# Reordering the loop body of four engine programs in an attention and low-rank feed-forward block

## Time and profile before

| | |
|---|---|
| median of 3 runs | 653.52 us |
| the profiled execution, its own time | 653.7 us |
| its span, first to last instruction | 651.7 us |
| mean granted TensorE clock, of full speed | 0.982 |
| PE busy | 608.7 us (93%) |
| DVE busy | 502.2 us (77%) |
| ACT busy | 418.3 us (64%) |
| POOL busy | 421.1 us (65%) |
| DMA, mean over the span | 32 GB/s |

### The profile page before, as it was taken

How to read it: one execution, slowest core, us unless ns; L and a number is a source line. 1 busy time by engine, 2 the same in 40 slices (tenths; PEclk the granted TensorE clock), 3 DMA queues, 4 the chain that set the end, 5 groups by cost and what they waited for, 6 DMA issues and landing times.

```text
span 651.7 us, 10353 instructions
## 1 busy us (share of the span) xinstructions
PE 608.7 (93%) x3437; PEld 522.9 (80%) x3437; DVE 502.2 (77%) x1093; ACT 418.3 (64%) x635; POOL 421.1 (65%) x363
## 2 busy tenths in 40 slices
PE   3699999999999999999999999999999999999996
PEld 1577878978798888878789788988798787987875
DVE  3457788797796968788796977968787877987567
ACT  0246685695668675695666856685756855677743
POOL 2745875677567765588566766587755785655664
PEclk9579999999999999999999999999999999999998
DMA  9201010210001000120002000020001200010001
GB/s 259 42 1 34 0 33 2 88 42 2 1 33 64 32 0 0 64 64 0 0 0 97 32 0 0 32 88 8 0 0 64 64 0 0 3 62 1 1 1 65
DMA packets 11745, 20.88 MB, mean 32 GB/s; under 512 B 3903, under 2 KB 7374, under 8 KB 11726
## 3 DMA queue, kind: packets, MB, share of 16 engines
q1 hardware_dynamic: 8144, 19.93, 8.8%
q10 hardware_dynamic: 3582, 0.70, 0.7%
HBM read 12.24 MB, written 8.39 MB: 32 GB/s over the span
## 4 chain that ended last, share of the span: by engine, by line
PE 45%; DVE 29%; ACT 10%; issue 8%; POOL 6%; ACTq 2%; DMA 1%; DVEq 0%; POOLq 0%
PE bank L1405 12%; PE bank L1411 6%; PE bank L1522 5%; PE bank L1577 5%; DVE fw L922 4%; DVE K L970 3%; PE bank L1497 3%; ACT fw L604 3%; PE bank L1478 3%; DVE st L892 2%; DVE hT L929 2%; POOL XNB L395 2%; PE bank L1488 2%; DVE XN L909 2%; DVE qT L977 2%
## 5 line engine op out<-in xcount | busy, mean ns | idle before, releaser
L252 POOL TENSOR_TENSOR gl<-fw,gh 128x512 fp32r<-128x512 f32 x80 | 106.4, 1335 | 60.5 <-ACT gh L609 59.5
L400 POOL TENSOR_TENSOR sqs<-fw 128x512 f32<-128x512 f32 x48 | 65.1, 1356 | 75.6 <-ACT fw L594 75.6
L604 ACT ACTIVATE fw<-fw,vec 128x512 f32<-128x512 f32 x96 | 76.1, 808 | 24.9 <-DVE fw L922 24.8
L594 ACT ACTIVATE fw<-bank,b1c 128x512 f32<-128x512 f32 x96 | 61.1, 685 | 41.5 <-PE bank L1411 40.5
L922 DVE SCALAR_TENSOR_TENSOR fw<-bank,b1c,rb 128x512 f32<-128x512 f32 x96 | 68.6, 743 | 12.4 <-ACT rb L600 12.4
L364 POOL TENSOR_TENSOR rsf<-vef,neghalf 128x4 f32<-128x4 f32 x48 | 51.3, 1069 | 33.0 <-DVE vef L915 32.9
L1533 PE MATMUL bank<-K,XN 128*128 128x256 f32 x256 | 61.8, 379 | 0.2 <-DVE K L970 0.2
L1577 PE MATMUL bank<-M,qT 128*128 128x256 f32 x256 | 60.7, 381 | 0.3 <-DVE qT L977 0.3
L364 POOL TENSOR_TENSOR rs<-ve,neghalf 128x2 f32<-128x2 f32 (+1 forms) x48 | 45.4, 945 | 24.1 <-DVE ve L1008 18.3
L609 ACT ACTIVATE gh<-fw 128x512 fp32r<-128x512 f32 x96 | 58.5, 625 | 1.6
L262 POOL TENSOR_TENSOR hTl<-hT,hTh 128x512 fp32r<-128x512 f32 x40 | 52.3, 1325 | 11.0 <-ACT hTh L613 10.8
(11 more groups left out here) (146 smaller groups left out, 1613.4 us busy)
## 6 DMA issues: line engine op xcount, KB each, us to landing
X<-in_L_attn_x_dram SPq DMA_DIRECT2D x16, 512.0 KB, 3.7
out_dram<-RES SPq DMA_DIRECT2D x14, 512.0 KB, 2.6
XNB<-in_L_ffn_qweights_dram SPq DMA_DIRECT2D x2, 512.0 KB, 7.9
out_dram<-RES SPq DMA_DIRECT2D x4, 256.0 KB, 2.1
RES<-in_L_ffn_qweights_dram SPq DMA_DIRECT2D x1, 512.0 KB, 9.7
Y<-in_L_ffn_lora_a_dram ACTq DMA_DIRECT2D x4, 96.0 KB, 6.2
Wp<-in_L_attn_Wq_dram SPq DMA_DIRECT2D x1, 256.0 KB, 6.1
Wp<-in_L_attn_Wk_dram SPq DMA_DIRECT2D x1, 256.0 KB, 7.2
```

What stands on the lines that cost most here:

```text
L252: engine.tensor_tensor(gl[:, h, m, :], fw[:, h, m, :], gh[:, h, m, :].bitcast(F32), ALU.subtract).then_inc(g_low[h][m], 1)
L400: pool.tensor_tensor(sqs[:, h, :], fw[:, h, 0, :], fw[:, h, 1, :], ALU.add).then_inc(sqs_ready[h], 1)
L594: act.activation(fw[:, h, m, :], FB[h][m][:], ACT.Square, bias=b1c[:, m, j:j + 1]).then_inc(sq_ready[h], 1)
L604: act.activation(fw[:, h, m, :], fw[:, h, m, :], ACT.Gelu, bias=lnb[:, m, j:j + 1], scale=lng[:, m, j:j + 1]).then_inc(g_ready[h], 1)
```

## The change

The order of the calls in `body` is changed on PE, DVE, ACT and POOL. `head` and `tail` keep their order, SP keeps all of its own, and no call is added, taken out or given to another engine. The table `BODY_USES` follows PE's new order. The diff, cut; lines that only serve as context are left out in places.

```diff
 BODY_USES
-    ("var", 1, 0), ("rs", 1, 0), ("q", 0, 1), ("q", 1, 0), ("q", 0, 0), ("var", 0, 1),
-    ("var", 1, 1), ("rs", 0, 1), ("rs", 1, 1), ("q", 1, 1), ("vk",), ("m",),
-    ("out", 0), ("var", 0, 2), ("xt", 0, 0), ("out", 1), ("rs", 0, 2), ("out", 2),
+    ("var", 1, 0), ("rs", 1, 0), ("q", 1, 0), ("q", 0, 1), ("q", 0, 0), ("var", 0, 1),
+    ("rs", 0, 1), ("var", 1, 1), ("rs", 1, 1), ("q", 1, 1), ("vk",), ("m",),
+    ("xt", 0, 0), ("out", 0), ("var", 0, 2), ("out", 1), ("rs", 0, 2), ("out", 2),
 POOL body
+                base_x(i, 1, BODY)
+                ffn_root(i, 1, 0)
                 base_xn(i, 0, BODY)
-                ffn_root(i, 1, 0)
-                base_x(i, 1, BODY)
...
                 h_lower(pool, i, 1, 0, 0)
+                add_squares(i, 0, 1)
                 h_lower(pool, i, 1, 0, 1)
-                add_squares(i, 0, 1)
+                ffn_root(i, 0, 1)
                 add_squares(i, 1, 1)
-                ffn_root(i, 0, 1)
+                ln1_root(i + 1, 0)
                 ffn_root(i, 1, 1)
                 base_xn(i, 1, BODY)
-                ln1_root(i + 1, 0)
                 g_lower(pool, i, 0, 1, 1)
+                g_lower(pool, i, 1, 1, 1)
                 g_lower(pool, i, 1, 1, 0)
-                g_lower(pool, i, 1, 1, 1)
 ACT body
-                k_exp(i, 0, BODY)
                 square(i, 0, 0, 0, BODY)
                 square(i, 0, 0, 1, BODY)
+                k_exp(i, 0, BODY)
...
                 gelu(i, 1, 0, 0)
+                gelu(i, 1, 0, 1)
                 g_higher(i, 0, 0, 1)
-                gelu(i, 1, 0, 1)
                 q_exp(i, 0, 0, BODY)
                 g_higher(i, 1, 0, 0)
                 g_higher(i, 1, 0, 1)
-                q_exp(i, 0, 1, BODY)
                 h_higher(i, 0, 0, 0)
                 h_higher(i, 0, 0, 1)
-                q_exp(i, 1, 0, BODY)
+                q_exp(i, 0, 1, BODY)
                 h_higher(i, 1, 0, 0)
                 h_higher(i, 1, 0, 1)
+                q_exp(i, 1, 0, BODY)
...
                 g_higher(i, 0, 1, 1)
+                gelu(i, 1, 1, 0)
+                gelu(i, 1, 1, 1)
                 g_copy(i)
-                gelu(i, 1, 1, 0)
                 g_higher(i, 1, 1, 0)
-                gelu(i, 1, 1, 1)
                 g_higher(i, 1, 1, 1)
+                q_exp(i, 1, 1, BODY)
                 h_higher(i, 0, 1, 0)
-                q_exp(i, 1, 1, BODY)
                 h_higher(i, 0, 1, 1)
                 h_higher(i, 1, 1, 0)
+                h_higher(i, 1, 1, 1)
                 m_copy(i, BODY)
-                h_higher(i, 1, 1, 1)
 DVE body
                 ffn_residual(i, 0, 0, 0)
+                ffn_residual(i, 0, 0, 1)
                 g_lower(dve, i, 1, 0, 1)
-                ffn_residual(i, 0, 0, 1)
...
-                ln1_statistics(i + 1, 0)
-                q_elu(i, 0, 1, BODY)
                 k_hat(i, 0)
                 k_hat(i, 1)
+                q_elu(i, 0, 1, BODY)
                 q_elu(i, 1, 0, BODY)
+                ln1_statistics(i + 1, 0)
+                k_hat(i, 2)
+                ffn_var(i, 0, 1, BODY)
+                ln1_mean_var(i + 1, 0)
+                ffn_normalise(i, 0, 1, 0, BODY)
+                k_hat(i, 3)
+                ffn_var(i, 1, 1, BODY)
+                ffn_normalise(i, 0, 1, 1, BODY)
                 ln1_statistics(i + 1, 1)
-                ffn_var(i, 0, 1, BODY)
-                ffn_var(i, 1, 1, BODY)
-                k_hat(i, 2)
-                ln1_mean_var(i + 1, 0)
-                k_hat(i, 3)
-                ffn_normalise(i, 0, 1, 0, BODY)
-                ffn_normalise(i, 0, 1, 1, BODY)
+                ffn_normalise(i, 1, 1, 0, BODY)
+                ffn_normalise(i, 1, 1, 1, BODY)
                 g_lower(dve, i, 0, 1, 0)
                 ln1_normalise(i + 1, 0, BODY)
-                ffn_normalise(i, 1, 1, 0, BODY)
+                ffn_residual(i, 0, 1, 0)
+                ffn_residual(i, 0, 1, 1)
+                q_elu(i, 1, 1, BODY)
+                block_diagonal(i, BODY)
                 ln1_mean_var(i + 1, 1)
-                ffn_normalise(i, 1, 1, 1, BODY)
-                ffn_residual(i, 0, 1, 0)
-                block_diagonal(i, BODY)
-                ffn_residual(i, 0, 1, 1)
                 ffn_residual(i, 1, 1, 0)
                 h_lower(dve, i, 0, 1, 0)
                 ffn_residual(i, 1, 1, 1)
-                q_elu(i, 1, 1, BODY)
                 ln1_normalise(i + 1, 1, BODY)
...
                 finish(i, 1)
-                xt_lower(dve, i + 1, 0, 1)
                 att_result(i, 2, BODY)
                 att_result(i, 3, BODY)
+                xt_lower(dve, i + 1, 0, 1)
+                xt_lower(dve, i + 1, 1, 0)
                 finish(i, 2)
                 finish(i, 3)
-                xt_lower(dve, i + 1, 1, 0)
 PE body
-                project_k(i, 0, BODY)
                 first_high(i, 0, 0, BODY)
                 first_low(i, 0, 0)
+                project_k(i, 0, BODY)
                 first_high(i, 1, 0, BODY)
+                variance(i, 0, 0, BODY)
                 first_low(i, 1, 0)
-                variance(i, 0, 0, BODY)
...
+                project_q(i, 1, 0, BODY)
                 project_q(i, 0, 1, BODY)
-                project_q(i, 1, 0, BODY)
...
                 first_low(i, 0, 1)
+                add_g(i, 0, BODY)
                 first_high(i, 1, 1, BODY)
+                add_g(i, 1, BODY)
+                variance(i, 0, 1, BODY)
                 first_low(i, 1, 1)
-                add_g(i, 0, BODY)
-                variance(i, 0, 1, BODY)
-                add_g(i, 1, BODY)
                 add_g(i, 2, BODY)
-                variance(i, 1, 1, BODY)
                 spread_rstd(i, 0, 1, BODY)
                 add_g(i, 3, BODY)
                 add_g(i, 4, BODY)
+                variance(i, 1, 1, BODY)
+                add_g(i, 5, BODY)
+                add_g(i, 6, BODY)
                 spread_rstd(i, 1, 1, BODY)
-                add_g(i, 5, BODY)
                 project_q(i, 1, 1, BODY)
-                add_g(i, 6, BODY)
                 add_g(i, 7, BODY)
...
                 make_m(i, BODY)
+                xt(i + 1, 0, 0, BODY)
                 first_high(i, 0, 2, BODY)
...
                 variance(i, 0, 2, BODY)
-                xt(i + 1, 0, 0, BODY)
...
                 rows_state(i, 3)
+                rows_low(i, 1)
                 rows_low(i, 0)
-                rows_low(i, 1)
+                rows_high(i, 2, BODY)
+                xt(i + 1, 1, 0, BODY)
                 rows_high(i, 3, BODY)
-                rows_high(i, 2, BODY)
+                rows_low(i, 3)
                 rows_low(i, 2)
-                rows_low(i, 3)
-                xt(i + 1, 1, 0, BODY)
```

More of the change, by code:

```diff
@@ L1217, in body @@
             def body(i):
+                k_elu(i, 0, BODY)
                 ffn_var(i, 0, 0, BODY)
-                k_elu(i, 0, BODY)
                 k_sum(i, 0)
@@ L1225, in body @@
                 ffn_var(i, 1, 0, BODY)
+                ffn_normalise(i, 0, 0, 1, BODY)
                 k_elu(i, 3, BODY)
-                ffn_normalise(i, 0, 0, 1, BODY)
                 k_sum(i, 2)
@@ L1262, in body @@
                 ffn_residual(i, 1, 1, 1)
-                q_elu(i, 1, 1, BODY)
                 ln1_normalise(i + 1, 1, BODY)
+                h_lower(dve, i, 1, 1, 0)
                 h_lower(dve, i, 1, 1, 1)
                 att_y(i, 0, BODY)
-                h_lower(dve, i, 1, 1, 0)
                 ffn_var(i, 0, 2, BODY)
+                xt_lower(dve, i + 1, 0, 0)
                 att_result(i, 0, BODY)
-                xt_lower(dve, i + 1, 0, 0)
                 att_y(i, 1, BODY)
```

## The result

The changed kernel takes 649.12 us (median of 4 runs, 648.84 to 649.56) against 653.2 us before (4 runs, 652.69 to 654.31). The ratio is 0.9936, 95% interval 0.9919 to 0.9953: faster by 0.64%. The forecast was 649.8. The profiled execution took 648.84 us; its span is 646.8 us, 4.9 us less than before.

What follows compares the result with a forecast made beforehand. PE, busy 93% of the span, was taken as the bound. Per turn -1.0 + 0.2 + 0.1 + 0.04 = -0.65 us, six turns -3.9, head and tail 0: 653.7 to 649.8 us; range 647.0 to 656.3.

Steps and rivals of the forecast that it cites:

- The ceiling of 2.4 us a turn: In the loop, a new order can give back at most PE's idle time, 75.20 - 72.76 = 2.4 us a turn.
- The 1.44 us stay: PE's wait in front of `spread_rstd(1, 0)`, behind a chain of 2.49 us on three engines, was to remain: 0.
- The wait ahead of `second_high(1, 1)`, -1.0 us: PE's wait there, caused by four `ln1_normalise` instructions on DVE ahead of `ffn_normalise(1, 1, 0)`, was to go: -1.0 us a turn.
- The new narrow places, +0.2 and +0.1 us a turn: Late `g_lower(1, 1, 0)` on POOL, +0.15 to +0.2; POOL's root for `spread_rstd(1, 1)`, +0.1; other new places 0.
- the slower rival: DVE and POOL exclusion holds `k_hat(2)` and `k_hat(3)`, delaying both `spread_rstd` of block 1: +1.05 us a turn, 660.0 us; chance 0.15.
- all new places hold: Rival: no new waits and late starts vanish too, -1.0 to -1.1 us a turn, 647.3 us; chance 0.10.
- the forecast's own term: The predicted net gain of one loop turn: -0.65 us.
- `q_exp` and its table load ahead of the roundings: On ACT, `q_exp(1, 1)` moved ahead of the `h_higher`; `block_diagonal` was to be done at 241.5, before `make_m` at 242.4: 0.
- The rival by the drain: Some 1.38 us of drain per table switch makes `make_m` 0.9 us late each turn: 655.2 us; chance 0.02.
- Head and tail 0: Outside the six loop turns, head and tail were to gain or lose nothing.
- its four terms: Per turn: -1.0 (`second_high(1, 1)`), +0.2 (`g_lower(1, 1, 0)`), +0.1 (`spread_rstd(1, 1)`), +0.04 (`second_high(1, 0)`), given as -0.65 us.

Runs made afterwards that it cites:

- The one move: Kernel before, with only DVE's two `ffn_normalise(1, 1, .)` put ahead of `ln1_normalise(i+1, 0)` and `ln1_mean_var(i+1, 1)`: 647.49 us, ratio 0.9905.
- the run with DVE's turn end as before: Changed kernel with DVE's `xt_lower(i+1, 0, 1)` and `xt_lower(i+1, 1, 0)` back at their old places at the turn's end: 648.47 us, ratio 0.992.
- the run with one rounding earlier: Kernel before with the DVE move and two `xt` moved on PE, plus ACT's `g_higher(1, 0, 0)` ahead of `q_exp(0, 0)`: 648.58 us, ratio 0.9932.
- the run with the fitted lists: Changed kernel with `project_k(3)` behind `variance(1, 0)`, POOL's tail `add_squares` ahead of `base_x`, and ACT, DVE, POOL lists refitted: 675.57 us, ratio 1.0364.

## Why the prediction was right

*What bounds the kernel.* Right: PE stays the busiest engine, in the loop at full clock, and the waits of PE led to the gain. The ceiling of 2.4 us a turn took PE's busy time as fixed, which it isn't quite: of the 0.9 us of a turn 0.3 came off it, with the same instructions.

*The 1.44 us stay.* Right: `variance(1, 0)` to `spread_rstd(1, 0)` is 2.49 us before and after (279.49 to 281.98). That they may be no free gain I had not said: filling the hole with `project_k(3)` made the kernel slower in both tries, and the trace has ACT's chain late by what the filler was late.

*The wait ahead of `second_high(1, 1)`, -1.0 us.* Right in place, cause and size: 3.81 to 2.76 us, -1.05. The one move shows the cause by itself.

*The new narrow places, +0.2 and +0.1 us a turn.* Too high. `g_lower(1, 1, 0)` ends at 314.41 and PE takes it at 314.50, a delay of 0.06 us (0.99 us from there to `make_m`, 0.93 before); POOL's root for `spread_rstd(1, 1)` ends at 305.98, PE comes at 306.26. `k_hat(0)` was estimated to start at 220.7 and end at 221.6; it stands at 293.74 and ends at 294.6, which is 220.7 and 221.5. The pair of `k_hat` took 2.58 us in all, not 3.06. So the exclusion between DVE and POOL was where I had put it, and the slower rival failed: `ffn_var(0, 1)` starts at 299.87 with 0.27 us of idle ahead of it. A turn gained 0.91 us, not 0.65, which is nearer to the rival "all new places hold" (1.0 to 1.1) than to the forecast's own term.

*`q_exp` and its table load ahead of the roundings.* Right: load at 311.81, Exp at 313.10, `block_diagonal` ends at 314.85, and `make_m` at 315.49 waits for nothing. The rival by the drain did not come: 0.02 us lies ahead of the load and 0.01 us between its end and the Exp. The Trainium skill ("ScalarE: Activation LUTs", What ACT_TABLE_LOAD costs) counts about 1.38 us of drain beside the load; the trace decides.

*Head and tail 0.* Wrong, and the one step of the walk that I had not taken. I moved DVE's `xt_lower` in thought and asked only whether PE gets them in time, not what stands beside them on POOL when the loop hands over to `tail`, whose lists are not those of the loop. At that seam the last turn of one profile has 1.03 us of wait, beside the `xt_lower`, and that of the other 1.70, where the output's transfer was late; how much of the latter is the change's stays open. And +0.48 us went at the first turn. In it `variance(1, 0, 0)` stands one low part nearer to its sum of squares and waits for it (0.17 us of idle at 124.02), and from the start of `first_high(1, 0)` to that of `project_k(1)` it is 4.12 us instead of 3.61. That the head's order makes the sum late there is a reading of the trace; no run tested it.

So the mechanism was right, and that the sum came out so near is luck: the steady state was worth 5.5 us (six turns of 0.91) where I had 3.9, and the ends took back about 1.5 where I had 0. Two errors of nearly the same size cancelled. The 649.8 of the forecast is 0.7 us off; the -0.95 us of the profiled head is in no term and is not the change's. A slip of the sum is too small to matter: its four terms give -0.66 a turn, not -0.65.

## What to carry to other kernels

When one engine is nearly always busy, list its idle places, and for each ask which call stands in front of the one that it waits for; here one move on another engine held all that the change won in a turn. Walk the new order also across the seams (head to loop, loop to tail), where two lists meet that were laid out apart. Before you fill a hole, ask who waits for the filler: `project_k(3)`, which ACT's chain needs, cost 1.0 us a turn, and two `xt`, put into the small holes, won 0.45. And two profiles of one kernel can differ at one place: the wait ahead of the tail was 1.0 us in one and 1.7 in the other.

## What the runs showed of the hardware

- DVE and POOL hold each other up, both ways. DVE's instructions of `k_rstd`, 0.23 to 0.29 us alone, took 1.28 to 1.40 beside POOL's `g_lower`, and POOL's `base_x` took 3.73 us instead of 2.4 beside two `xt_lower` of DVE. The one that waits gets in when the other's instruction ends: twice an `xt_lower` that started beside `base_x` (568.64 and 568.74) ended 0.55 us behind it. So a row of short DVE instructions beside a full POOL queue went at POOL's pace, one for one. Not all are held: DVE's L1031, which has one operand in a PSUM bank, took 1.28 us for two beside `base_x` (567.45) and as much without it (569.94 in the run with DVE's turn end as before).
- PE's clock. The 1.44 us of idle in each turn left it at its full level, 2.4 GHz (1.00 in both windows above). With 2.0 us of idle in each turn it fell in four turns of six (0.61 on average over the 4.4 us behind the wait) and stayed at 1.00 in the other two. Behind 1.32 and 1.44 us of idle within 4 us it fell to 1.2 GHz (0.51 on average from 577.25 to 580.70), and the first pair of matmuls of L1544 took 1.0 us instead of 0.54 (577.92 to 578.92); behind 1.05 and 1.44 us it didn't fall (the run with one rounding earlier). In the run with the fitted lists PE was idle for 2.9 us in each turn, and only the first turn has a mean below 1.00 (0.98). So a wait can cost more than its length, but these runs give no length from which it does.
